# An FFN with per-sequence low-rank adapters: the index on GpSimd's queue, the first loads dealt over two queues, the indexed loads in halves

## The reference

```python
# block 1, "cond": LoRA with the adapter of each sequence, rank 16, 16 adapters, SCALE 0.5
def lora_add(base, inp, A, B):
    t = einsum('bri,bni->bnr', A[layer_idx][lora_indices], inp)
    return base + einsum('bor,bnr->bno', B[layer_idx][lora_indices], t) * SCALE
gate = lora_add(x @ W_gate.T, x, A_gate, B_gate)      # 512 -> 1376
up   = lora_add(x @ W_up.T,   x, A_up,   B_up)
y    = lora_add(act @ W_down.T, act, A_down, B_down)   # act = silu(gate) * up; 1376 -> 512
# block 2, "ffn": RMS norm, 512 -> 1792 -> 512
nx = y * rsqrt(mean(y**2) + 1e-5) * ln_w
return x + (silu(nx @ gate_w.T) * (nx @ up_w.T)) @ down_w.T
```

## Time and profile before

| | |
|---|---|
| median of three runs | 425.59 us (423.69 to 425.59) |
| profiled execution | 426.08 us, its span 424.2 us |
| mean granted TensorE clock | 0.987 |
| PE busy | 407.9 us, 96% of the span, 1850 matmuls |
| PEld busy (weight loads, beside PE) | 338.0 us, 80% |
| DVE busy | 320.0 us, 75% |
| ACT busy | 234.7 us, 55% |
| POOL busy | 12.7 us, 3% |
| DMA | 31.86 MB, mean 75 GB/s |

### The profile page before, as it was taken

How to read it: one execution, slowest core, us unless ns; L and a number is a source line. 1 busy time by engine, 2 the same in 40 slices (tenths; PEclk the granted TensorE clock), 3 DMA queues, 4 the chain that set the end, 5 groups by cost and what they waited for, 6 DMA issues and landing times.

```text
span 424.2 us, 5436 instructions
## 1 busy us (share of the span) xinstructions
PE 407.9 (96%) x1850; PEld 338.0 (80%) x1850; DVE 320.0 (75%) x489; ACT 234.7 (55%) x369; POOL 12.7 (3%) x16
## 2 busy tenths in 40 slices
PE   8977949999999999999999999999999999999996
PEld 6868737888888888888888888888888888888885
DVE  3578775968686756656579988787878869899993
ACT  4468845565656356761374665535455567375730
POOL 6300000000000110000000000000000000000000
PEclk9998979999999999999999999999999999999999
DMA  7630204231111132030010112132312042405112
GB/s 258 176 112 0 77 1 136 72 110 49 51 49 51 50 124 76 0 100 0 0 51 0 50 51 98 52 105 88 105 50 99 2 136 89 148 1 168 68 50 99
DMA packets 14092, 31.86 MB, mean 75 GB/s; under 512 B 2290, under 2 KB 4594, under 8 KB 14066
## 3 DMA queue, kind: packets, MB, share of 16 engines
q1 hardware_dynamic: 13200, 29.96, 22.1%
q10 hardware_dynamic: 866, 1.57, 1.0%
HBM read 29.43 MB, written 2.10 MB: 74 GB/s over the span
## 4 chain that ended last, share of the span: by engine, by line
PE 87%; DVE 4%; issue 3%; ACT 3%; DMA 1%; ACTq 0%; DVEq 0%
PE bank L1303 42%; PE bank L1628 16%; PE bank L1493 14%; PE bank L1411 5%; PE bank L1506 2%; PE bank L1313 2%; PE bank L1439 2%; ACT stack L395 2%; DMA wraw<-w_in 1%; PE bank L1456 1%; PE bank L1447 1%; DVE stack L819 1%; DVE xsum_c L1077 1%; DVE act L862 0%; PE bank L1513 0%
## 5 line engine op out<-in xcount | busy, mean ns | idle before, releaser
L1303 PE MATMUL bank<-xs,ws 128*128 128x512 f32 x840 | 197.8, 395 | 6.3 <-ACT bank L395 6.0
L1303 PEld LDWEIGHTS bank<-xs,ws 128*128 128x128 f32 x840 | 158.3, 190 | 40.3 <-ACT bank L395 6.5
L1493 PE MATMUL bank<-xs,wdc 128*128 128x512 f32 x264 | 62.9, 390 | 0.0
L1493 PEld LDWEIGHTS bank<-xs,wdc 128*128 128x128 f32 x264 | 49.3, 188 | 10.1
L395 ACT ACTIVATE xs<-act 128x512 fp32r<-128x512 f32 x71 | 43.0, 624 | 21.2 <-DVE act L969 7.6
L819 DVE TENSOR_TENSOR xs<-act,xs 128x512 fp32r<-128x512 f32 x71 | 47.6, 687 | 4.7 <-ACT xs L395 4.2
L819 DVE TENSOR_TENSOR ws<-wraw,ws 128x256 fp32r<-128x256 f32 (+2 forms) x48 | 32.4, 682 | 15.2 <-ACT ws L395 15.1
L1628 PE MATMUL bank<-xs,vs 128*128 128x512 f32 x168 | 38.2, 390 | 0.0
L395 ACT ACTIVATE bank<-bank 128x512 f32<-128x512 f32 x22 | 12.7, 580 | 45.5 <-PE bank L1303 45.5
L1628 PEld LDWEIGHTS bank<-xs,vs 128*128 128x128 f32 x168 | 31.5, 188 | 6.5
L395 ACT ACTIVATE ws<-wraw 128x256 fp32r<-128x256 f32 (+2 forms) x47 | 28.6, 619 | 11.8 <-PE bank L1303 4.1
(11 more groups left out here) (124 smaller groups left out, 441.4 us busy)
## 6 DMA issues: line engine op xcount, KB each, us to landing
wraw<-wgu_in SPq DMA_DIRECT2D x22, 512.0 KB, 3.3
wdr<-vs_in SPq DMA_DIRECT2D x7, 512.0 KB, 3.5
wdr<-wd_in SPq DMA_DIRECT2D x11, 256.0 KB, 2.7
wraw<-vj_in SPq DMA_DIRECT2D x3, 896.0 KB, 4.6
xa<-xT_in SPq DMA_DIRECT2D x3, 512.0 KB, 6.1
wraw<-w_in ACTq DMA_DIRECT2D x4, 256.0 KB, 6.4
bgu_raw<-bgu_in SPq DMA_DIRECT2D x32, 32.0 KB, 1.9
xres<-xT_in SPq DMA_DIRECT2D x4, 256.0 KB, 3.8
```

The source lines that it names most:

```text
L1303: ins = mm(z[:, :], ws[:, j % 2, w, s, k * P:(k + 1) * P], xs[:, c, r, k, :], start=(start and k == 0 and s == 0 and r == 0), stop=(k == 1 ...
L1493: ins = mm(z[:, :], wd[:, s, h * P:(h + 1) * P], x[r], start=(start and s == 0 and r == 0), stop=False, skip_group_check=True)
```

## The change

SP's first loads become x0_0, x0_1, w0_2, x0_3 and then both halves of xa1; ScalarE's become w0_0, w0_1, (the wait and the small silu), x0_2, w0_3, wsh. The index is loaded by GpSimd, as its first instruction. Behind SP's wait for the index, agu and chunk 0 of the stack come in halves: agu 0 to 3, stack 0 to 3, agu 4 to 7, stack 4 to 7, each half with a semaphore of its own. ScalarE's and VectorE's orders are changed too: xa1 ahead of agu, x_sum 1 and 2 and lo_t(0, 0) ahead of t_mask(0), stack(0, 1) before short(0)'s results are used (on ScalarE) and behind t_lo(0) (on VectorE), x_sum 3 behind t_mask(1). TensorE's program is the same. The diff in full:

```diff
@@ -208,8 +208,9 @@
         s_maskr = sem("mask_repeated")
         s_act_pad, s_pad, s_pad_d = sem("short_act_padding_zero"), sem("padding_zero"), sem("down_lora_padding_zero")
         s_table = sem("table_touched")
-        s_x0_ld, s_x1_ld = [sem(f"x_half_0_loaded_{k}") for k in range(3)], [sem(f"x_half_1_loaded_{k}") for k in range(2)]
-        s_w0_ld, s_wsh_ld, s_agu_ld = [sem(f"first_w_loaded_{k}") for k in range(KT)], sem("short_w_loaded"), sem("agu_loaded")
+        s_x0_ld, s_x1_ld = [sem(f"x_half_0_loaded_{k}") for k in range(KT)], [sem(f"x_half_1_loaded_{k}") for k in range(2)]
+        s_w0_ld, s_wsh_ld = [sem(f"first_w_loaded_{k}") for k in range(KT)], sem("short_w_loaded")
+        s_agu_ld, s_raw0_ld = ([sem(f"{w}_loaded_half_{t}") for t in range(2)] for w in ("agu", "bgu_0"))
         s_w_ld = [sem("w_loaded_even"), sem("w_loaded_odd")]
         s_raw_ld = [sem("bgu_loaded_0"), sem("bgu_loaded_1")]
         s_wd_ld = [sem("wd_loaded_even"), sem("wd_loaded_odd")]
@@ -275,25 +276,30 @@
             def load_stack(c):
                 if c >= 2:
                     sp.wait_ge(s_stklo, 2 * (c - 2) + 2)
-                first = sum(CHUNK[:c])
                 for b in range(B):
-                    row = RANK * (b % 2)
-                    sp.dma_start(raw[c % 2][row:row + RANK, b // 2, 0:CHUNK[c]],
-                                 bgu_in[ds(which[b], 1), :, first:first + CHUNK[c]].rearrange("o r m -> (o r) m")
-                                 ).then_inc(s_raw_ld[c % 2], 16)
+                    load_stack_of(c, b, s_raw_ld[c % 2])
+
+            def load_stack_of(c, b, loaded):
+                row, first = RANK * (b % 2), sum(CHUNK[:c])
+                sp.dma_start(raw[c % 2][row:row + RANK, b // 2, 0:CHUNK[c]],
+                             bgu_in[ds(which[b], 1), :, first:first + CHUNK[c]].rearrange("o r m -> (o r) m")
+                             ).then_inc(loaded, 16)
 
             sp.dma_start(xa0[:, 0, :], xT_in[0, :, 0, :]).then_inc(s_x0_ld[0], 16)
             sp.dma_start(xa0[:, 1, :], xT_in[0, :, 1, :]).then_inc(s_x0_ld[1], 16)
-            sp.dma_start(xa0[:, 2:4, :], xT_in[0, :, 2:4, :]).then_inc(s_x0_ld[2], 16)
+            sp.dma_start(w0_raw[:, 2], w0_in[2]).then_inc(s_w0_ld[2], 16)
+            sp.dma_start(xa0[:, 3, :], xT_in[0, :, 3, :]).then_inc(s_x0_ld[3], 16)
+            for k in range(2):
+                sp.dma_start(xa1[:, 2 * k:2 * k + 2, :], xT_in[1, :, 2 * k:2 * k + 2, :]).then_inc(s_x1_ld[k], 16)
             sp.wait_ge(s_idx, 16)
             which = []
-            for b in range(B):
-                which.append(sp.value_load(idx[0:1, b:b + 1], min_val=0, max_val=R - 1))
-                sp.dma_start(agu_raw[:, b], agu_in[ds(which[b], 1)].rearrange(
-                    "o p (g k r) -> (o p) g k r", g=2, k=KT)).then_inc(s_agu_ld, 16)
-            for k in range(2):
-                sp.dma_start(xa1[:, 2 * k:2 * k + 2, :], xT_in[1, :, 2 * k:2 * k + 2, :]).then_inc(s_x1_ld[k], 16)
-            load_stack(0)
+            for t in range(2):
+                for b in range(4 * t, 4 * t + 4):
+                    which.append(sp.value_load(idx[0:1, b:b + 1], min_val=0, max_val=R - 1))
+                    sp.dma_start(agu_raw[:, b], agu_in[ds(which[b], 1)].rearrange(
+                        "o p (g k r) -> (o p) g k r", g=2, k=KT)).then_inc(s_agu_ld[t], 16)
+                for b in range(4 * t, 4 * t + 4):
+                    load_stack_of(0, b, s_raw0_ld[t])
             load_w(2)
             load_stack(1)
             load_w(3)
@@ -370,6 +376,7 @@
 
         @block.gpsimd
         def _(pool):
+            pool.dma_start(idx[:, :], idx_in[:, :]).then_inc(s_idx, 16)
             m = mask[0:64, :].rearrange("p (b n) -> p b n", b=4)
             nc.gpsimd.memset(mask[0:64, :], LORA_SCALE).then_inc(s_mask, 1)
             pool.wait_ge(s_mask, 1)
@@ -469,8 +476,10 @@
                 silu(part, part, 1.0 if j < S1 else -1.0).then_inc(s_s22, 1)
 
             def stack_hi(c, t):
-                if t == 0:
-                    a.wait_ge(s_raw_ld[c % 2], 16 * B * (c // 2 + 1))
+                if c == 0:
+                    a.wait_ge(s_raw0_ld[t], 16 * 4)
+                elif t == 0:
+                    a.wait_ge(s_raw_ld[c % 2], 16 * B * ((c + 1) // 2))
                     if c == 2:
                         a.wait_ge(s_uu, 4)
                     elif c >= 3:
@@ -647,54 +656,54 @@
                 copy(lora_a(0, b), agu_raw[:, b]).then_inc(s_agu_hi, 1)
 
             load_w0(0)
-            nc.scalar.dma_start(idx[:, :], idx_in[:, :]).then_inc(s_idx, 16)
+            load_w0(1)
             a.wait_ge(s_warm, 2)
             silu(stat[:, 1:2], stat[:, 0:1]).then_inc(s_table, 1)
-            for k in range(1, KT):
-                load_w0(k)
+            nc.scalar.dma_start(xa0[:, 2, :], xT_in[0, :, 2, :]).then_inc(s_x0_ld[2], 16)
+            load_w0(3)
             nc.scalar.dma_start(wsh_raw, wsh_in).then_inc(s_wsh_ld, 16)
             for k in range(KT):
                 if k >= 1:
                     a.wait_ge(s_w0_ld[k], 16)
                     copy(w0(0, k), w0_raw[:, k]).then_inc(s_w0hi, 1)
-                if k < 3:
-                    a.wait_ge(s_x0_ld[k], 16)
+                a.wait_ge(s_x0_ld[k], 16)
                 copy(xs[:, (X11, X21)[k // 2], 0, k % 2, :], xa0[:, k, :]).then_inc(s_xhi[0], 1)
             a.wait_ge(s_wsh_ld, 16)
             for q in range(2):
                 copy(wsh_w[0][:, :, q, :], raw_kg[:, :, q, :]).then_inc(s_wsh_hi, 1)
-            a.wait_ge(s_agu_ld, 16 * B)
-            for b in range(4):
-                hi_agu(b)
             a.wait_ge(s_x1_ld[0], 16)
             hi_x(0, X12, xa1[:, 0:2, :])
             a.wait_ge(s_x1_ld[1], 16)
             hi_x(0, X22, xa1[:, 2:4, :])
+            a.wait_ge(s_agu_ld[0], 16 * 4)
+            for b in range(4):
+                hi_agu(b)
             stack_hi(0, 0)
             a.wait_ge(s_xsum[0], 1)
             hi_x(0, T_SLOT[0], xsum_c[:, 0])
+            a.wait_ge(s_xsum[0], 2)
+            hi_x(0, T_SLOT[1], xsum_c[:, 1])
+            stack_hi(0, 1)
             a.wait_ge(s_short, 1)
+            a.wait_ge(s_agu_ld[1], 16 * 4)
             for b in range(4, B):
                 hi_agu(b)
             t_hi(0)
-            a.wait_ge(s_xsum[0], 2)
-            hi_x(0, T_SLOT[1], xsum_c[:, 1])
+            hi_a(2)
             unit_silu(0)
             unit_silu(1)
             short_silu(0)
-            stack_hi(0, 1)
-            hi_a(2)
             t_neg()
+            stack_hi(1, 0)
             hi_b(2)
             t_hi(1)
-            stack_hi(1, 0)
+            stack_hi(1, 1)
             a.wait_ge(s_short, 2)
             a.wait_ge(s_xsum[0], 3)
             hi_x(0, T_SLOT[2], xsum_c[:, 2])
             unit_silu(2)
             unit_silu(3)
             short_silu(1)
-            stack_hi(1, 1)
             a.wait_ge(s_xsum[0], 4)
             a.wait_ge(s_uu, 4)
             hi_x(0, XT4, xsum_c[:, 3])
@@ -1101,40 +1110,40 @@
             for q in range(2):
                 v.wait_ge(s_wsh_hi, q + 1)
                 sub(wsh_w[1][:, :, q, :], raw_kg[:, :, q, :], wsh_w[0][:, :, q, :]).then_inc(s_wsh_lo, 1)
+            lo_x(0, XC["12"], xs[:, X12, 1], xa1[:, 0:2, :], xs[:, X12, 0])
+            lo_x(0, XC["22"], xs[:, X22, 1], xa1[:, 2:4, :], xs[:, X22, 0])
             for b in range(4):
                 lo_agu(b)
-            lo_x(0, XC["12"], xs[:, X12, 1], xa1[:, 0:2, :], xs[:, X12, 0])
             v.wait_ge(s_mask, 3)
             nc.vector.tensor_copy(mask[96:P, 256:CH], mask[32:64, 256:CH]).then_inc(s_maskr, 1)
-            lo_x(0, XC["22"], xs[:, X22, 1], xa1[:, 2:4, :], xs[:, X22, 0])
             v.wait_ge(s_wsh_lo, 2)
             x_sum(0, 0)
+            x_sum(0, 1)
             stack_lo(0, 0)
-            x_sum(0, 1)
+            lo_t(0, 0)
+            x_sum(0, 2)
             v.wait_ge(s_maskr, 1)
             t_mask(0)
             for b in range(4, B):
                 lo_agu(b)
-            lo_t(0, 0)
+            lo_t(0, 1)
             t_lo(0)
-            lo_t(0, 1)
+            stack_lo(0, 1)
             unit_mul(0)
             unit_mul(1)
             short_act(0)
             sums(2)
-            x_sum(0, 2)
-            stack_lo(0, 1)
             lo_a(2)
+            lo_b(2)
             t_mask(1)
-            lo_b(2)
+            x_sum(0, 3)
             t_lo(1)
+            stack_lo(1, 0)
             lo_t(0, 2)
-            stack_lo(1, 0)
             unit_mul(2)
             unit_mul(3)
             short_act(1)
             stack_lo(1, 1)
-            x_sum(0, 3)
             lo_t(0, 3)
 
             def group(j, first, last):
```

## The result

The changed kernel took 413.98 us (median of 4 runs, 413.71 to 414.19) against 424.82 us for the one before (4 runs, 423.69 to 425.59): ratio 0.9746, 95% interval 0.9718 to 0.9775, so 10.8 us or 2.5% less. The forecast was 412.0, range 409.2 to 417.0; the narrower band that the prediction gave a chance of 0.67 was 410 to 413.4, and the measurement lies 0.6 us above it. The profiled execution took 413.84 us with a span of 411.9; the one of before was 426.08 with 424.2, so between the two traces there are 12.2 us to explain. The profiled execution of before was on the slow side of its runs, which is why the medians are only 10.8 apart.

A forecast was written before the change was run, and what follows sets the result against it. Two TensorE gaps in the first 60 us (4.77 and 6.05) and the half clock behind them were taken as the loss. 426.08 less 14.4 (11.5 + 2.9) is 411.7, plus 0.3 for thin places: 412.0, range 409.2 to 417.

The forecast's parts named there:

- eighteen products behind it: TensorE's products from p6(0) on: at full clock 4.11 us instead of 7.03, 2.9 us gained.
- late front: Rival at the first loads: xa1's megabyte or a late index delays agu's first half 2 to 4 us; 413.5 to 416, chance 0.15.
- signs named for being right: Trace: short(0) 17.5 to 18, first_loras(0) 28.9 to 29.6, short(1) 0.8 behind loras, p6(0) 47 to 48, clock 1.00, waits under 2.
- The mechanism: TensorE's 4.77 and 6.05 us gaps before p6(0) go, the clock stays up, and the gain lasts to the end.
- The new stall of 0.8 us at short(1): short(1) waits for unit_mul(0), now behind stack_lo(0,1) on VectorE: 0.8 us of new stall, start at 31.6.
- the landing of the short weights: First loads: beside xa1's 1 MB they land up to 1 us later, at 10.6 to 11.6; ScalarE takes them at 11.4.
- agu behind xa1 has taken: Front, before short(0): processing agu after xa1 uses up the slack; thinnest place of the front, short(0) about 17.7.
- The other rule of that page that I weighed: First loads: several engines share 16 DMA engines, saving only issue time; by it the 0.3 us gain is 0, time 412.3.
- The index: GpSimd's load, issued near 0.5 us, lands between 2.4 and 4.5; SP starts agu at 6.0, as before.
- All behind p6(0) is TensorE's own work: After p6(0) TensorE waits for nothing, so what is gained by then stays to the end.
- the 0.3 us of slack that I gave ca(0): ScalarE's ca(0) done at 47.1, p6(0) starting at 47.4 with no gap: 0.3 us of slack.
- 14.4 us of forecast gain: Total gain: p6(0) 11.5 us earlier, at 47.4 from 58.94, plus 2.9 us from faster products behind it.

The follow-up runs named there:

- before_warm_gap: Kernel before, plus 24 matmuls on ones between g(0) and p6(0) to keep TensorE working through its gap: 423.53 us, ratio 0.9950.
- loads_only: Changed kernel's new loads with ScalarE's and VectorE's orders of the kernel before: 419.90 us, ratio 0.9905 to the kernel before.
- orders_only: Changed kernel's ScalarE and VectorE orders with the loads of the kernel before: 420.16 us, ratio 0.9909 to the kernel before.
- xa1_behind_wait: Changed kernel with both loads of xa1 behind SP's wait for the index instead of ahead: 416.00 us, ratio 0.9812 to the kernel before.
- idx_on_act: Changed kernel with the index load back on ScalarE's queue, second as before: 415.36 us, ratio 0.9780 to the kernel before.
- first_loads_dealt_as_before: Changed kernel with first tokens all on SP's queue (x0_2 joined with x0_3), first weights all on ScalarE's: 415.40 us, ratio 0.9774 to the kernel before.
- mixed kernels: Changed kernel with ScalarE's and VectorE's old orders up to short_silu(0): 413.50 us; also with the next weights' sums ahead of lo_t(0, 3): 412.84 us.
- mixed_orders: Changed kernel's loads and later orders, but ScalarE's and VectorE's orders up to short_silu(0) as before: 413.50 us, ratio 0.9722 to the kernel before.

## Why the prediction was right, and by how much each step missed

| step | forecast | measured |
|---|---|---|
| short weights taken by ScalarE | 11.4 | 12.74 |
| SP issues agu | 6.0 | 8.87 |
| short(0) starts | 17.7 | 18.67 |
| stack's second half lands | 21 | 23.2 |
| first_loras(0) starts | 29.1 | 30.52 |
| short(1) starts, behind the loras' end | 31.6, 0.8 | 33.02, 0.83 |
| p6(0) starts | 47.4 | 48.7 |
| eighteen products behind it | 4.1 | 4.4 |
| p4(0)'s wait | none | 0.8 |

**The number is in the range, but not where I put the most weight.** 413.98 is above the 410 to 413.4 that had 0.67, and inside the 413.5 to 416 of the rival "late front". Half of that rival came: it was xa1's megabyte, and short(0) started 0.97 us late. But it was to act through agu landing late, and ScalarE took agu at 16.12 with no wait; it acted through the short weights. Of the signs named for being right, the granted clock of 1.00 and short(1) at 0.8 behind the loras' end came; short(0) (18.67 for 17.5 to 18), first_loras(0) (30.52 for 28.9 to 29.6) and p6(0) (48.7 for 47 to 48) were late, and TensorE's waits were 2.8 us in sum without the one for the first data, not under 2. The misses all go one way; none made up for another.

**The mechanism held.** Both long gaps went, the loras and the products behind them ran at full clock, and what was gained by p4(0) (12.2 us) stayed to the end. before_warm_gap shows the clock's part by itself and loads_only and orders_only which half of the change does what. The new stall of 0.8 us at short(1) behind stack_lo(0,1) came as worked out.

**The first term that was mis-sized is the landing of the short weights.** I let xa1's megabyte make them up to 1 us later and then charged nothing, because ScalarE took them at 11.4 before. They came at 12.74, 1.3 later and 1.1 behind the latest landing that I allowed, and short(0) 1.0 later than forecast. I had reckoned with bytes per microsecond of the whole pipe; xa1_behind_wait shows that it was xa1, and the rows of the changed kernel from 8 to 10 us, where xa1 runs beside the short weights (rows of 3 KB), show that SP's queue with its 4 KB rows takes more than half of it:

```profile
q1 hardware_dynamic: 161, 0.49, 60.5%
q10 hardware_dynamic: 164, 0.34, 43.9%
```

The late landing costs this much only in the new order. In loads_only, with agu ahead of xa1 on both engines, the short weights came at 13.13 and short(0) started without a wait: the slack that "agu behind xa1 has taken", in the prediction's words, is what the landing then needed. By the Trainium skill's page "DMA: Bandwidth & Descriptors", section "Queues, rings and completion order", each DMA engine takes turns between queues by packets. The counts agree where both queues are full (223 and 214, 161 and 164; what the profile counts here are mostly single rows of 2 to 4 KB, while the page's packet holds several descriptors), not from 4 to 6 us in idx_on_act (262 and 134). What the prediction lacked was to multiply them by their size. The other rule of that page that I weighed, that starting loads from several engines only saves issue time, would have dealt as before make no difference, and it cost 1.1 to 1.4 us; that kernel also joins x0_2 and x0_3 into one load with wide rows, and the two were not tried apart.

**The index was off by 2.9 us, and it mattered little.** A GpSimd load took 6.6 us to land from 1.30; I had taken 2 to 4 from 0.5. t_hi(0) started at 27.04 with t_mask(0) done at 26.86, so all of the late stack's cost is 0.2 us of the 1.4 at first_loras(0); the rest is VectorE's chain, begun late by the short weights (0.97), and its steps between, 0.1 to 0.2 longer than my sum.

**Behind p6(0) a step was missing.** "All behind p6(0) is TensorE's own work" was true of the trace before because ScalarE and VectorE had 6 us of TensorE's standing to prepare group 0's sums. With the gap filled, VectorE is still at lo_t(0, 3) when the sums are wanted, and 0.8 us is given back at p4(0). I had asked what is late next only up to p6(0). And at p6(0) itself the 0.3 us of slack that I gave ca(0) was not there: it ended with g(0), and in the mixed kernels, where TensorE comes earlier, p6(0) waits 0.43 to 0.44 us for it.

**The frame.** 14.4 us of forecast gain less 1.3 at p6(0), less 0.3 at the eighteen products, less 0.8 at p4(0), leaves 12.0 of the 12.2 between the two profiled executions. The other 1.4 between 12.2 and 10.8 is that the profiled execution of before (426.08) lay above its median; I named 0.5 for it in words and did not take it off in the sum; with it the forecast would have been 411.5, further off. The kernel before spreads over 423.7 to 426.7 in all its runs here, the changed one over 413.7 to 415.2. That the wider spread comes from the clock's fall and rise at two gaps fits the mixed kernels, but was not tested on the kernel before.

## What to carry to other kernels

When a gap is filled, write down what the helping engines did in it: the next place where TensorE needs them is the next wait. In the stretches where both queues were full they shared by packets, so put short rows beside what is urgent and wide rows behind it, and count the packets and not only the bytes. A reordering that a change brings along should be tried apart from its loads: here the late half of it gave a whole gap and the early half cost a microsecond.

## What the runs showed of the hardware that was not expected

- A gap of TensorE of 4.8 to 6 us was followed by a granted clock of 0.50: 2.7 us more for eighteen products (7.03 against 4.37 with the gap filled by idle matmuls). A gap of 2.93 us was followed by slow loras too (2.63 against 1.70) and by 0.50, gaps of 2.04 and 2.14 at short(0) (idx_on_act, first_loads_dealt_as_before) and of 0.8 by none. Ahead of the first data a pause of 1.87 was followed by a stretch at 0.50, pauses of 1.74 and 1.66 by none.
- The recorded clock can't be relied on at the start. mixed_orders has slow first matmuls, 17 in 5.86 us against 24 in 5.79, and 1.00 beside them; and in the changed kernel the ten matmuls on ones take 4.54 us, 0.45 each, beside a recorded 1.00, where later ones of the same size take 0.23. There the durations have to be read.
- An index of 32 bytes loaded through GpSimd's queue took 6.5 to 6.9 us to land beside full queues.
- Two full queues moved equal numbers of packets in the same time, and bytes by their size: 0.52 MB against 0.30. Behind the small index load ScalarE's queue moved fewer for a microsecond: 37 packets against 159.
